# Part of the state update of a selective scan moved from GpSimd to TensorE: dt·u·B of two states, and D·u, as products with diagonal matrices

## What is computed

```python
u   = silu(conv1d(ctx @ in_proj.T) + conv_b)          # 4 x 512 channels x 512 steps
dt_low, B, C = split(x_proj @ u, [16, 32])            # 16 rows each
dt  = softplus(dt_proj @ dt_low + dt_bias)
for each step t and state n of 16:
    h_n = h_n * exp(dt * A_n) + (dt * u) * B_n        # a scan over t
    y  += h_n * C_n
y   = (y + D * u) * silu(layernorm(x))
x   = x + tanh(g_x) * y
xn  = layernorm(x)
h   = silu(bitlinear(xn, w_gate)) * bitlinear(xn, w_up)
out = x + tanh(g_f) * bitlinear(h, w_down)
```

## Time and profile before

| | |
|---|---|
| median of three runs | 626.79 us |
| the profiled execution | 631.2 us, its span 629.4 us |
| busy: DVE, POOL, ACT, PE | 564.6, 519.7, 510.8, 506.5 us |
| mean granted TensorE clock | 0.964 |
| time from one `gated_y` to the next, s = 8 to 11 | 35.36, 30.56, 30.79, 30.91 us |

### The profile page before, as it was taken

How to read it: one execution, slowest core, us unless ns; L and a number is a source line. 1 busy time by engine, 2 the same in 40 slices (tenths; PEclk the granted TensorE clock), 3 DMA queues, 4 the chain that set the end, 5 groups by cost and what they waited for, 6 DMA issues and landing times. The chain is left out here.

```text
span 629.4 us, 9210 instructions
## 1 busy us (share of the span) xinstructions
PE 506.5 (80%) x3014; PEld 340.2 (54%) x3014; DVE 564.6 (90%) x777; ACT 510.8 (81%) x761; POOL 519.7 (83%) x286
## 2 busy tenths in 40 slices
PE   6999665766767788888868787888787978799997
PEld 2443354755655565556545555565455655564553
DVE  1899989999997899999999999999989999987564
ACT  3869789886995898978697989877879898778784
POOL 1568799999999799999999999999999999941000
PEclk9999879789796999999999999999899999999999
DMA  8991930710840010117501101066101010000001
GB/s 298 398 411 61 357 141 33 267 51 1 311 182 9 0 52 2 33 34 274 196 33 34 35 34 35 33 237 211 56 33 35 34 34 19 1 17 18 18 18 50
DMA packets 29985, 64.47 MB, mean 102 GB/s; under 512 B 3681, under 2 KB 11873, under 8 KB 26866
## 3 DMA queue, kind: packets, MB, share of 16 engines
q1 hardware_dynamic: 29938, 63.89, 28.1%
HBM read 55.75 MB, written 8.13 MB: 101 GB/s over the span
## 5 line engine op out<-in xcount | busy, mean ns | idle before, releaser
L755 POOL TENSOR_TENSOR area_s<-area_s,b_bc 128x1024 f32<-128x1024 f32 x128 | 300.5, 2364 | 13.8 <-DVE u_all L1317 7.8
L438 PE MATMUL pY<-ident,area_s 128*128 128x128 f32 x640 | 102.1, 285 | 82.1 <-DVE area_s L1325 78.9
L438 PEld LDWEIGHTS pY<-ident,area_s 128*128 128x128 f32 x640 | 72.8, 144 | 109.8 <-DVE area_s L1325 79.1
L1317 DVE TENSOR_TENSOR_SCAN area_s<-pA,area_s 128x512 f32<-128x512 f32 x96 | 114.5, 1206 | 4.8 <-ACT pA L1001 4.1
L1001 ACT ACTIVATE pA<-dt_all,a_neg 128x512 f32<-128x512 f32 x160 | 107.6, 681 | 13.3 <-DVE area_s L1317 12.3
L481 PE MATMUL pG<-wq_gu,area_f 128*128 128x512 fp8e4 x448 | 107.8, 384 | 3.5 <-ACT area_f L951 2.8
L747 POOL TENSOR_TENSOR u_all<-u_all 128x1024 f32<-128x1024 f32 x44 | 103.9, 2361 | 0.2 <-DMA u_all<-bc_rows 0.2
L1325 DVE TENSOR_TENSOR area_s<-area_s,pC 128x512 f32<-128x512 f32 x144 | 95.5, 665 | 6.4 <-issue 3.8
L432 PE MATMUL pC<-ident,xdT 128*128 128x128 f32 x576 | 91.9, 287 | 3.5 <-DVE area_s L1325 2.3
L432 PEld LDWEIGHTS pC<-ident,xdT 128*128 128x128 f32 x576 | 71.0, 145 | 11.1 <-DVE area_s L1325 9.0
L481 PEld LDWEIGHTS pG<-wq_gu,area_f 128*128 128x128 bf16 x448 | 41.7, 98 | 51.4 <-issue 4.3
(11 more groups left out here) (197 smaller groups left out, 979.8 us busy)
## 6 DMA issues: line engine op xcount, KB each, us to landing
b_bc<-bc_rows SPq DMA_DIRECT2D x16, 1024.0 KB, 9.4
area_s<-x SPq DMA_DIRECT2D x32, 256.0 KB, 3.0
u_all<-bc_rows SPq DMA_DIRECT2D x14, 512.0 KB, 7.4
b_bc<-w_gate SPq DMA_DIRECT2D x1, 4096.0 KB, 14.6
dt_all<-x SPq DMA_DIRECT2D x1, 4096.0 KB, 24.9
area_f<-w_up SPq DMA_DIRECT2D x1, 4096.0 KB, 34.3
area_f<-w_down SPq DMA_DIRECT2D x1, 4096.0 KB, 15.0
out<-area_f SPq DMA_DIRECT2D x16, 256.0 KB, 2.0
```

The lines of the kernel that those rows point to most:

```text
L438: mm = pe.matmul(pY[:, k * P:(k + 1) * P], src[:, k * P:(k + 1) * P], ident[:, :], is_transpose=True, start=(first and k == 0), stop=(last ...
L755: gp.tensor_tensor(db[c % NDB], du[s % 2].rearrange("p (a l) -> p a l", a=1).to_broadcast([P, CH, L]), b_bc[:, CH * c:CH * c + CH, :], ALU ...
L1317: dve.tensor_tensor_scan(h, exp_bank(s, n), db[(n // CH) % NDB][:, n % CH, :], 0.0, ALU.mult, ALU.add).then_inc(S["s_scan"], 1)
```

## The change

From unit 4 on dt·u·B of pair 2 (states 4 and 5) is no longer made by GpSimd. TensorE transposes dt·u (`du_transpose`), ScalarE copies it to SBUF (`copy_duT`), and TensorE multiplies it, 128 time steps at a time, by a diagonal matrix that holds B's values (`db_state`), into the PSUM bank that would have held the exponential. ScalarE writes these two exponentials into the free pair buffer in SBUF instead, and the scan takes its two operands from the other side. The diagonals (two states, four blocks) are made by ScalarE once a batch (`diagonals`), eight instructions of 128x128, in the last unit of the batch before: units 3, 7, 11. D·u becomes, in all units, a product of u with a diagonal of D (`skip` is now 128x128, `y_skip` a real matmul). B's rows 4 and 5 are not loaded after the first batch. In units with a first tile, TensorE's order around gate chunk 2 is changed.

```diff
+def pool_pairs(s):
+    return [c for c in range(NCH) if s < PLAIN or c != PE_PAIR]      # PE_PAIR = 2
 load_u(s):
-                past(sp, S["s_skip"], s - 1)
+                past(sp, S["s_skd"], s - 1)
 y_skip(s):
+                past(pe, S[f"d_u{s % 2}"], (s // 2) * 16)
                 pe.wait_ge(S["s_skip"], s + 1)
-                y_part(du_skip, first=(s >= PLAIN)).then_inc(S["s_skd"], 1)
+                for k in range(NT):
+                    mm = pe.matmul(pY[:, k * P:(k + 1) * P], u_in[s % 2][:, k * P:(k + 1) * P], diag_d[:, :], ...)
+                mm.then_inc(S["s_skd"], 1)
+            def du_transpose(s):
+                pe.wait_ge(S["s_du"], s + 1)
+                pe.wait_ge(S["s_szT"], s)
+                for k in range(NT):
+                    mm = pe.transpose(pT[:, k * P:(k + 1) * P], du[s % 2][:, k * P:(k + 1) * P], ident[:, :])
+                mm.then_inc(S["s_dup"], 1)
+            def db_state(s, i):
+                n = CH * PE_PAIR + i
+                pe.wait_ge(S["s_duT"], s - PLAIN + 1)
+                pe.wait_ge(S["s_diag"], CH * NT * (s // NT - 1) + NT * (i + 1))
+                pe.wait_ge(S["s_scan"], s * NS + n - 2)
+                for k in range(NT):
+                    mm = pe.matmul(exp_bank(s, n)[:, k * P:(k + 1) * P], duT[:, k, :], diag_b[i][:, k, :], start=True, stop=True)
+                mm.then_inc(S["s_dbp"], 1)
 TensorE, unit s:
-                fill(s, 0, 1)
+                du_transpose(s)
                 if s > PLAIN:
                     y_sum(s - 1, 15)
                     y_sum_pooled(s - 1, 3)
                 c_bcast(s, 2)
-                fill(s, 1, 2)
+                fill(s, 0, 1)
+                db_state(s, 0)
+                db_state(s, 1)
                 y_skip(s)
                 y_sum(s, 2)
                 c_bcast(s, 3)
-                fill(s, 2, 4)
+                fill(s, 1, 4)
...
-                y_sum_pooled(s, 1)
-                c_bcast(s, 10)
-                y_sum(s, 7)
-                if t1 % NT == 0:
-                    c_bcast(s, 11)
-                    y_sum(s, 10)
-                gate(t1, 2)
-                gate(t1, 3)
-                if t1 % NT:
-                    c_bcast(s, 11)
-                    y_sum(s, 10)
+                if t1 % NT:
+                    y_sum_pooled(s, 1)
+                    c_bcast(s, 10)
+                    y_sum(s, 7)
+                    gate(t1, 2)
+                    gate(t1, 3)
+                    c_bcast(s, 11)
+                else:
+                    c_bcast(s, 10)
+                    y_sum(s, 7)
+                    y_sum_pooled(s, 1)
+                    gate(t1, 2)
+                    c_bcast(s, 11)
+                    gate(t1, 3)
+                y_sum(s, 10)
 GpSimd, unit s:
-                    times_b(s + 1, 2)
 ScalarE:
 exponential(g):
+                if by_pe(s, n):
+                    act.wait_ge(S["s_scan"], (s - 1) * NS + CH * (PE_PAIR + NDB) + CH)
+                    act.activation(db[PE_PAIR][:, n % CH, :], dt_all[:, s, :], ACT.Exp, scale=a_neg[:, s % NT, n:n + 1]).then_inc(S["s_exp"], 1)
+                    return
 skip(s):
-                act.activation(du_skip, u_in[s % 2], ACT.Copy, scale=d_raw[:, s % NT:s % NT + 1]).then_inc(S["s_skip"], 1)
+                act.activation(diag_d[:, :], ident[:, :], ACT.Copy, scale=d_raw[:, s % NT:s % NT + 1]).then_inc(S["s_skip"], 1)
+            def copy_duT(s):
+                act.wait_ge(S["s_dup"], s - PLAIN + 1)
+                past(act, S["s_dbp"], CH * (s - PLAIN))
+                act.activation(duT.rearrange("p k d -> p (k d)"), pT[:, :], ACT.Copy).then_inc(S["s_duT"], 1)
+            def diagonals(b, i):
+                if b == 1:
+                    act.wait_ge(S["s_dbu"], db_count(PLAIN - 1, PE_PAIR))
+                else:
+                    act.wait_ge(S["s_dbp"], CH * (b * NT - 1 - PLAIN) + i + 1)
+                n = CH * PE_PAIR + i
+                for k in range(NT):
+                    act.activation(diag_b[i][:, k, :], ident[:, :], ACT.Copy, scale=xdT[:, b, k, n:n + 1]).then_inc(S["s_diag"], 1)
 plain units, step n:
+                    if s == 3 and n in (13, 15):
+                        diagonals(1, n // 2 - 6)
 unit s, step n:
+                    if s == PLAIN and n == 0:
+                        copy_duT(s)
+                    if n in (8, 9) and s % NT == NT - 1 and s + 1 < UNITS:
+                        diagonals(s // NT + 1, n - 8)
+                    if n == 15 and s + 1 < UNITS:
+                        copy_duT(s + 1)
 VectorE, scan(s, n):
+                if by_pe(s, n):
+                    dve.wait_ge(S["s_dbp"], CH * (s - PLAIN) + n % CH + 1)
+                    at, dbu = dbu, at
```

More of the change, by code:

```diff
@@ L69, with db_count, by_pe @@
 BN_AT = [sum(own_stats(i) for i in range(t)) for t in range(UNITS + 1)]
+PE_PAIR = 2
+def pool_pairs(s):
+    return [c for c in range(NCH) if s < PLAIN or c != PE_PAIR]
+DB_AT = [sum(len(pool_pairs(i)) for i in range(s)) for s in range(UNITS + 1)]
+def db_count(s, c):
+    return DB_AT[s] + pool_pairs(s).index(c) + 1
+def by_pe(s, n):
+    return s >= PLAIN and n // CH == PE_PAIR
 VE, RR, M2, REC1, XS, SS, RH, M3, REC2, FAC, MH, XSUM, DEV = range(13)
@@ L81 @@
     d_xz0 d_xz1 d_xr0 d_xr1 d_bbc0 d_bbc1 d_bbc2 d_bbc3 d_c0 d_c1 d_c2 d_c3 d_u0 d_u1 d_out0 d_out1
-    s_exp s_dbu s_scan s_mul s_pmul s_pytr s_cb s_ytr s_du s_skip s_skd s_sz s_szp s_szT s_y s_x1
+    s_exp s_dbu s_scan s_mul s_pmul s_pytr s_cb s_ytr s_du s_skip s_skd s_dup s_duT s_diag s_dbp s_sz s_szp s_szT s_y s_x1
     f_bn f_sum f_dev f_ve f_rr f_xn f_xs f_e f_xm f_xqp f_xqT f_gate f_silu f_up f_h f_sq f_mh f_rh f_hs f_hm
@@ L119, in build @@
         ones = sb("ones", [P, P])
+        diag_d = sb("diag_d", [P, P])
         neg_half = sb("neg_half", [P, UNITS])
@@ L165, in build @@
         du = [carve(area_s, 7168 + L * i, L) for i in range(2)]
-        du_skip = carve(area_s, 8192, L)
+        duT = carve(area_s, 8192, L).rearrange("p (k d) -> p k d", k=NT)
+        diag_b = [b_bc[:, CH * PE_PAIR + i, :].rearrange("p (k l) -> p k l", k=NT) for i in range(CH)]
         xz = [carve(area_s, 8704 + L * i, L) for i in range(2)]
@@ L272, in load_b @@
                 for q in quarters:
-                    past(sp, S["s_dbu"], (b * NT - 1) * NCH + 2 * q + 2)
-                    sp.dma_start(b_bc[:, 4 * q:4 * q + 4, :], bc_rows[b, 4 * q:4 * q + 4, :].partition_broadcast(P)).then_inc(S[f"d_bbc{q}"], 16)
+                    if b:
+                        sp.wait_ge(S["s_dbu"], db_count(b * NT - 1, 2 * q + 1))
+                    first = 4 * q + (CH if b and 2 * q == PE_PAIR else 0)
+                    sp.dma_start(b_bc[:, first:4 * q + 4, :], bc_rows[b, first:4 * q + 4, :].partition_broadcast(P)).then_inc(S[f"d_bbc{q}"], 16)
             def store(t):
@@ L458, in y_skip @@
                     pe.wait_ge(S["s_y"], s)
+                past(pe, S[f"d_u{s % 2}"], (s // 2) * 16)
                 pe.wait_ge(S["s_skip"], s + 1)
-                y_part(du_skip, first=(s >= PLAIN)).then_inc(S["s_skd"], 1)
+                for k in range(NT):
+                    mm = pe.matmul(pY[:, k * P:(k + 1) * P], u_in[s % 2][:, k * P:(k + 1) * P], diag_d[:, :],
+                                   start=(s >= PLAIN and k == 0), stop=False, skip_group_check=True)
+                mm.then_inc(S["s_skd"], 1)
[13 more added lines that the diff above has]
+                mm.then_inc(S["s_dbp"], 1)
             def z_transpose(s):
@@ L518, in down @@
                     past(pe, S["f_o"], t)
-                    pe.wait_ge(S["s_szT"], z_done)
+                    if z_done < UNITS:
+                        pe.wait_ge(S["s_duT"], z_done - PLAIN + 1)
+                    else:
+                        pe.wait_ge(S["s_szT"], z_done)
                 for k in range(part * DK, min(part * DK + DK, FK)):
@@ L525, in keep_on @@
             def keep_on(s):
-                pe.wait_ge(S["s_szT"], s)
+                pe.wait_ge(S["s_duT"], s - PLAIN + 1)
                 for k in range(NT):
@@ L739, in dt_u @@
                 past(gp, S[f"d_u{s % 2}"], (s // 2) * 16)
-                past(gp, S["s_dbu"], s * NCH - NCH)
+                past(gp, S["s_dbu"], DB_AT[max(s - 1, 0)])
                 gp.wait_ge(S["k_dt"], 1 if s == 0 else UNITS)
@@ L751, in times_b @@
                     gp.wait_ge(S["s_du"], s + 1)
-                if c % 2 == 0:
+                if c % 2 == 0 or c == PE_PAIR + 1:
                     gp.wait_ge(S[f"d_bbc{c // 2}"], (s // NT) * 16 + 16)
@@ L781, in _ @@
                         dt_u(s + 1)
-                    if n in (9, 11, 13, 15):
+                    if n in (9, 11, 13, 15) and (n - 9) // 2 in pool_pairs(s + 1):
                         times_b(s + 1, (n - 9) // 2)
@@ L1305, in scan @@
                 dve.wait_ge(S["s_exp"], s * NS + n + 1)
-                if n % CH == 0:
-                    dve.wait_ge(S["s_dbu"], s * NCH + n // CH + 1)
```

(8 more changed lines are left out.)

2 lines of the change are left out of this document (1 added, 1 removed).

## The result

The changed kernel takes 635.07 us (median of four, 634.17 to 639.56) against 626.97 before: a ratio of 1.0125, with a 95% interval of 1.0089 to 1.0161. I had forecast slower, but only by 2.2 us (629.0, range to 633.5); it is 8.1 us slower and outside the range.

A forecast was written before the change was run, and what follows sets the result against it. VectorE was taken as the bound in plain units. Terms +0.1 (units 3 and 4), +0.9 (second and third units), +4.4 (fourth) and -3.2 (first) made +2.2 us: 629.0 us against the median, range 624.3 to 633.5.

The forecast's parts named there:

- `y_skip` is 0.44 longer beside it: Plain units: VectorE is the bound, so the longer D·u product on TensorE costs nothing.
- units 3 and 4 at +0.1: Units 3 and 4 together: 1.6 us lost to diagonals against 1.5 gained by row 10 passing the pooled sum.
- The diagonals' +1.6: Unit 3, n = 13 and 15: ScalarE's diagonals make exponential 2 of unit 4 ready near 183.0, 1.6 us lost.
- the base: Sum of +2.2 us from a profiled execution of 631.2 us, laid on the median of 626.79: 629.0 us.
- the fourth units: Units 7 and 11: ScalarE's eight diagonals delay SiLUs and exponentials, scan 14 waits 2.2 us more each; +4.4 for two.
- Rival 1: Fourth units: the eight diagonals fit in ScalarE's idle 5.9 us, 4.4 falls to 0, time 624.6 us; chance 0.18.
- the first units: Units 8 and 12: new TensorE order and SiLUs 0.8 us earlier through GpSimd, -1.6 each, -3.2 together.
- loads of weights overlap the passes: TensorE's added products: weight loads do not lengthen the passes, so four products of two passes take 0.87 us.
- Rival 4: TensorE, each unit: loads do not overlap passes, 2.6 us becomes 5.2; +22, 651 us; chance 0.05.
- The copy as a new wait: ScalarE's copy of dt·u ahead of exponential 2: 0.15 us a unit in six second and third units, +0.9.
- rival 3: Late copy of dt·u: ScalarE's work comes 0.4 us later than VectorE needs in nine units; +3.6, 632.6 us; chance 0.16.
- Rival 2: Unit 4: added products keep TensorE at 2.4 GHz, -3.0 us at most, 626.0 us; chance 0.14.

The follow-up runs named there:

- second trace: The kernel before, unchanged, run and traced again: 627.5 us median of ten runs, ratio 0.9987; the traced execution took 627.71 us.

## Why the prediction was wrong

- **Wrong: "In plain units VectorE is the bound and `y_skip` is 0.44 longer beside it: nothing."** VectorE waits for `gated_y` behind the last sum, and `y_skip` is directly ahead of that sum. I had no row of a plain unit's `gated_y` from which to take the work as hidden. It costs 0.35 at a plain unit's end at the high clock and 1.73 where the clock was low (taking it out: 2.4 us less in the median; alone: 2.2 more). The low clock is 1.4 of unit 2's +1.85.
- **Wrong: units 3 and 4 at +0.1.** Measured +2.4. The diagonals' +1.6 was right for unit 3 (+1.64). What I set against it was 1.5 from the new order at the low clock of the earlier trace rows. That clock was not there in every execution: in the other trace of before unit 4 has 0.65 us of waiting at C's row 10, not 3.37, and the order gives 0.5 us where the gates run at the high clock. And the sum has no term for the chain behind the diagonals (the product, the sum, the transposes of dt·u, the first copy). At the low clock it took from 182.74 to 186.1, scan 3 came 1.20 us late and the product with C's row 3 0.81 late; at the high clock only the second wait is left (0.71).
- **Wrong: the base.** Differences in units 3 and 4 were taken from an execution 4.4 us above the median, and then the sum was laid on the median. I saw the 4.4 and did not ask which unit held it; by the second trace, unit 4 held 2.7 of it.
- **Right: the fourth units**, +2.1 each by ScalarE's diagonals, forecast +2.2. The wait is not at scan 14, where I had put it and looked for it in the next profile, but at scan 11 and at C's row 11. Rival 1 (the diagonals hide) is out where the change puts them; at n = 4 they do hide. What I did not foresee is the clock falling behind the hole they make, 1.4 us more in some executions.
- **Right in kind, mis-sized: the first units**, -1.33 for -1.6. The relief of GpSimd and the order do not add up in full: 0.54 and 1.06 make 1.33, because both shorten the wait for C's row 10. `residual` of unit 12 starts 1.95 us behind `gated_y`'s start instead of 3.88, which is the 2 us that I expected.
- **Right: loads of weights overlap the passes.** The eight passes of a state's `db_state` take 0.89 us from its start to the next one's in the changed kernel, 0.11 a pass, forecast 0.87:

```profile
408.81 1.05 PE L506 MATMUL pC<-b_bc,area_s 128*128 128x128 f32 x8
409.70 1.06 PE L506 MATMUL pA<-b_bc,area_s 128*128 128x128 f32 x8
```

The rule of the Trainium skill (TensorE: Matmul & The Clock Gate, on packing small matmuls) that loads overlap only where the row group differs does not hold here: the same rows, and no time added. A pass over 128 columns with a load of its own takes 0.11 us, a quarter of the 0.43 that the prediction has for 512 columns. Rival 4 is out.

- **The copy as a new wait** cost nothing in second and third units (+0.1 for six, forecast +0.9), so rival 3 is out as well. Unit 13 alone shows 0.4, with a wait of 0.31 for an exponential; I did not follow it.
- Rival 2 (the clock holds in unit 4) came true in a way I had not thought of: unit 4 of the changed kernel has a mean clock of 0.98, and the kernel before has 0.92 there in its second trace. That most of its executions are like this one is inferred from their times; only two were traced.

## What to carry to other kernels

Work that is moved to an engine with idle time is free only at the place where that engine stands: eight small ScalarE instructions cost 2.1 us a unit at n = 8 and 9 and nothing at n = 4. Before a work item is called hidden, look at what it stands directly ahead of, in each kind of unit and not only in the most frequent one, and at the low clock too where the clock varies. And before differences are taken from one profiled execution, compare its time with the median; where they are apart, find the unit that holds the difference first.

## What the chip showed that I had not expected

The granted clock of TensorE differs between executions of the same code at the same place, by 1 to 3 us of time: unit 4 of the kernel before takes 32.56 or 35.30 us. Unit 2 takes 28.72 or 27.34 in two kernels that are alike up to unit 4, and unit 7 with late SiLUs 33.00 or 34.41 in two that differ only in unit 4. A short stand of 1.47 us had a stretch at 1.2 GHz behind it in one execution and none in the profiled one of the changed kernel; filling idle time with transposes did not keep the clock up. A 128x512 scan whose two operands change places between SBUF and PSUM took 1.21 us in the changed kernel (at 189.09), as before.
